# Gated cross-attention and mixture-of-experts block: three hand-written schedules re-ordered, and the running sum of softmax weights cut differently

## What is computed

```python
x = x + tanh(g_xattn) * cross_attention(layernorm(x), context)   # x: 4 x 512 x 512
x = x + tanh(g_ffn)   * moe_ffn(layernorm(x))
# cross_attention: q, k, v are linear maps, q and k RMS-normalised, 16 heads of 32;
#   two softmaxes, over 1344 text rows and over 257 image rows of the context,
#   their results summed, then a linear map
# moe_ffn: 8 experts (512 -> 2*256 -> 512), the two best of each token, weighted,
#   plus one shared expert (512 -> 2*1024 -> 512)
```

## Time and profile before

| | |
|---|---|
| median of 3 runs | 1726.33 us (1725.85 to 1728.0) |
| the profiled execution | 1728.0 us, its span from first to last instruction 1726.7 us |
| granted PE clock over the span | 0.997 |
| DVE busy | 1201.3 us (70%) |
| ACT busy | 822.3 us (48%) |
| POOL busy | 901.7 us (52%) |
| the DMA engines | 53% of the span, 158 GB/s |

### The profile page before, as it was taken

One profiled execution on the slowest core, in us unless ns is written; L12 is line 12 of the kernel. 1 busy time (PEld: TensorE's weight loads), 2 busy tenths in 40 slices (PEclk: granted clock), 3 DMA queues, 4 the chain that ended last, 5 costly groups with the idle time before them and its releaser, 6 DMA issues. The chain is left out here.

```text
span 1726.7 us, 24755 instructions
## 1 busy us (share of the span) xinstructions
PE 1689.0 (98%) x8694; PEld 1105.9 (64%) x8694; DVE 1201.3 (70%) x2250; ACT 822.3 (48%) x1520; POOL 901.7 (52%) x343
## 2 busy tenths in 40 slices
PE   6999999999999999999999999998999999999999
PEld 5888878885444445444544444445777778888777
DVE  6776677667888887888778888877555354443565
ACT  4433333236666664666556666662322355554221
POOL 3221312116777774787747777711515477675542
PEclk9999999999999999999999999999999999999999
DMA  9556858546555542554545445221313488876533
GB/s 330 165 165 196 229 182 211 180 164 192 138 151 146 145 134 57 147 151 132 148 122 127 111 131 142 84 93 42 134 37 134 159 266 271 261 264 211 166 109 98
DMA packets 198603, 273.04 MB, mean 158 GB/s; under 512 B 30968, under 2 KB 128008, under 8 KB 197964
## 3 DMA queue, kind: packets, MB, share of 16 engines
q1 hardware_dynamic: 192928, 254.61, 50.0%
q0 software_dynamic: 5120, 16.78, 2.9%
q10 hardware_dynamic: 432, 0.07, 0.0%
HBM read 198.15 MB, written 106.18 MB: 176 GB/s over the span
## 5 line engine op out<-in xcount | busy, mean ns | idle before, releaser
L1255 ACT ACTIVATE P<-ps 128x512 f32<-128x512 f32 (+1 forms) x832 | 444.4, 596 | 257.2 <-PE ps L1096 223.0
L640 DVE TENSOR_REDUCE mp<-ps 128x1 f32<-128x448 f32 x768 | 426.9, 613 | 83.9 <-PE ps L443 83.9
L1521 POOL TENSOR_TENSOR sacc<-sacc,P 128x2048 f32<-128x2048 f32 x90 | 396.3, 4403 | 17.5 <-ACT P L1255 6.9
L443 PE MATMUL ps<-Kst,Qst 96*128 96x448 f32 (+1 forms) x1024 | 382.6, 391 | 2.0 <-DVE mp L640 1.0
L443 PEld LDWEIGHTS ps<-Kst,Qst 96*128 96x128 f32 x1024 | 192.4, 188 | 210.8 <-DVE mp L640 150.5
L1096 PE MATMUL ps<-Qst,Kst 100*128 100x512 f32 (+1 forms) x832 | 321.2, 410 | 3.2 <-ACT P L1255 2.3
L1039 PE MATMUL ps<-P,Vg 128*32 128x512 f32 (+2 forms) x1664 | 216.2, 606 | 0.3 <-ACT P L1255 0.2
L822 POOL TENSOR_TENSOR cl<-craw,ch 128x1024 fp32r<-128x1024 f32 (+2 forms) x26 | 62.1, 2387 | 283.2 <-ACT ch L550 283.2
L1096 PEld LDWEIGHTS ps<-Qst,Kst 100*128 100x128 f32 (+1 forms) x832 | 151.8, 185 | 61.6 <-ACT P L1255 37.3
L49 PE MATMUL ps<-W,ch 128*128 128x512 f32 (+1 forms) x408 | 162.5, 398 | 0.0
L51 PE MATMUL ps<-W,cl 128*128 128x512 f32 (+1 forms) x408 | 159.7, 391 | 0.0
(11 more groups left out here) (245 smaller groups left out, 3072.0 us busy)
## 6 DMA issues: line engine op xcount, KB each, us to landing
gur<-in_w_gate_up SPq DMA_DIRECT2D x23, 1024.0 KB, 7.5
Kst<-KHd SPq DMA_DIRECT2D x56, 320.0 KB, 4.8
Vd<-vf SPq DMA_DIRECT2D x50, 256.0 KB, 2.1
craw<-in_ctxT SPq DMA_DIRECT2D x24, 512.0 KB, 4.5
KHd<-sth SPq DMA_DIRECT2D x24, 512.0 KB, 3.5
KLd<-stl SPq DMA_DIRECT2D x24, 512.0 KB, 4.8
dnr<-in_w_down SPq DMA_DIRECT2D x23, 512.0 KB, 3.9
xg<-Xg SPq DMA_DIRECT2D x23, 512.0 KB, 7.7
```

The lines of the kernel that those rows point to most:

```text
L443: pe.matmul(ps[:, bank, 0:c1 - c0], Qst[G % 3][0:96, j, 128 * qt:128 * qt + 128], Kst[G % 2][0:96, j, c0:c1], start=True, stop=True).then_ ...
L640: dve.reduce_max(out, ps[:, bank, 0:c1 - c0], AX.X).then_inc(d_ra, 1)
L1255: act.activation(P[slot(G, kt)][:m, j, :], ps[:m, 2 + (e - 1) % 3, :], ACT.Exp, scale=SCALE).then_inc(a_exp, 1)
L1521: pool.tensor_tensor(sacc[:, h], sacc[:, h], P[slot(G, kt)][:, h], ALU.add).then_inc(g_sum, 1)
```

## The change

- **Start of the projection.** On ACT, `weight_high` of the text keys' weights moves from `i = 1` to `i = 0`, ahead of `q_norm(0)`; that of the values' weights moves from ahead of `q_norm(2)` to behind `q_norm(1)`. On DVE, `ln_finish` and `centred` stand ahead of `q_add` in every iteration, and two `ln_stats` move behind `q_scale` and one iteration earlier.
- **Units.** One unit moves from step 7 to step 2 of each group.
- **Running sum.** POOL's first addition is one operation over four heads, not two over two heads each, and waits for the whole of tile 1; POOL adds two heads of tile 7 and DVE the other two (three and one before).
- **Feed-forward.** `gu_low` is four operations in place of one, `dn_low` two; the counts that others wait for follow. POOL no longer waits for `choose(3)` before `gu_low(3)` nor for the last `products` before `gu_low(4)`, and `dn_low(3)` stands behind `scatter(3)`.

```diff
@@ act_project, loop over i
             if i == 0:
                 chunk_high(0)
-            if i in (1, 2):
-                weight_high(i, s_wt[i - 1], W[:, 1, i - 1, 0], wraw[:, 1, i - 1, 1])
+                weight_high(1, s_wt[0], W[:, 1, 0, 0], wraw[:, 1, 0, 1])
             if i in (1, 3, 5, 9):
                 ln_root({1: 2, 3: 3, 5: 4, 9: 5}[i])
             if i < NT:
                 q_norm(i)
+            if i == 1:
+                weight_high(2, s_wt[1], W[:, 1, 1, 0], wraw[:, 1, 1, 1])
@@ dve_project, loop over i
             if i + 1 < NT:
                 x_low(i + 1)
-            if 1 <= i < NT:
-                q_add(i)
-            if 1 <= i < 7:
-                ln_stats(2 * i + 2)
-                ln_stats(2 * i + 3)
             if i + 3 < NT:
                 if i in (1, 3, 5, 9):
                     ln_finish({1: 2, 3: 3, 5: 4, 9: 5}[i])
                 centred(i + 3)
+            if 1 <= i < NT:
+                q_add(i)
             if i < NT:
                 q_variance(i)
             if 0 <= u < NU:
                 k_add(u)
             if i < NT:
                 q_scale(i)
+            if i < 6:
+                ln_stats(2 * i + 4)
+                ln_stats(2 * i + 5)
@@ attention
-    UNITS = (7, 6, 3, 6, 5, 6, 6, 6, 6, 5, 6, 2, 0)
+    UNITS = (7, 6, 4, 6, 5, 6, 6, 5, 6, 5, 6, 2, 0)
...
     def sum_no(G, kt):
-        return 8 * G + max(1, kt) + 1
+        return 7 * G + max(1, kt)
@@ dve_attend
-        def add_head_of_7(G):
+        def add_half_of_7(G):
             dve.wait_ge(a_exp, exp_no(G, 7, 3))
             dve.wait_ge(g_sum, sum_no(G, 6))
-            dve.tensor_tensor(sacc[:, 3:4], sacc[:, 3:4], P[slot(G, 7)][:, 3:4], ALU.add).then_inc(d_add, 1)
+            dve.tensor_tensor(sacc[:, 2:4], sacc[:, 2:4], P[slot(G, 7)][:, 2:4], ALU.add).then_inc(d_add, 1)
@@ pool_attend
-        def first_sum(G):
-
-            if G:
-                pool.wait_ge(p_tot, 5 * (G - 1) + TEXT_TOTAL)
-            for j in (0, 2):
-                pool.wait_ge(a_exp, exp_no(G, 1, j + 1))
-                h = slice(j, j + 2)
-                pool.tensor_tensor(sacc[:, h], P[slot(G, 0)][:, h], P[slot(G, 1)][:, h], ALU.add).then_inc(g_sum, 1)
-
         def add(G, kt):
             pool.wait_ge(a_exp, exp_no(G, kt, 3))
-            pool.wait_ge(g_sum, sum_no(G, kt) - 1)
-            h = slice(0, 3 if kt == 7 else 4)
-            pool.tensor_tensor(sacc[:, h], sacc[:, h], P[slot(G, kt)][:, h], ALU.add).then_inc(g_sum, 1)
+            if kt == 1:
+                if G:
+                    pool.wait_ge(p_tot, 5 * (G - 1) + TEXT_TOTAL)
+            else:
+                pool.wait_ge(g_sum, sum_no(G, kt) - 1)
+            h = slice(0, 2 if kt == 7 else 4)
+            pool.tensor_tensor(sacc[:, h], (P[slot(G, 0)] if kt == 1 else sacc)[:, h], P[slot(G, kt)][:, h], ALU.add).then_inc(g_sum, 1)
...
-            if G < NG - 1 and kt == 2:
-                first_sum(G)
-            if G < NG - 1 and 3 <= kt < 9:
+            if G < NG - 1 and 2 <= kt < 9:
                 add(G, kt - 1)
@@ pool_ffn
         def gu_low(q):
             pool.wait_ge(a_gu, q)
-            pool.tensor_tensor(gul[q % 2], gur[raw_slot(q)][:], guh[q % 2].bitcast(F32), ALU.subtract).then_inc(g_gu, 1)
+            for k in range(4):
+                pool.tensor_tensor(gul[q % 2][:, k], gur[raw_slot(q)][:, k], guh[q % 2][:, k].bitcast(F32), ALU.subtract).then_inc(g_gu, 1)
 
         def dn_low(q):
             pool.wait_ge(a_dn, q)
-            pool.tensor_tensor(dnl[q % 2], dnr[raw_slot(q)][:], dnh[q % 2].bitcast(F32), ALU.subtract).then_inc(g_dn, 1)
+            for k in range(2):
+                pool.tensor_tensor(dnl[q % 2][:, k], dnr[raw_slot(q)][:, k], dnh[q % 2][:, k].bitcast(F32), ALU.subtract).then_inc(g_dn, 1)
...
         scatter(2)
-        pool.wait_ge(d_run, 17)
         gu_low(3)
+        scatter(3)
         dn_low(3)
-        scatter(3)
-        pool.wait_ge(d_al, 16)
         gu_low(4)
```

More of the change, by code:

```diff
@@ L1428, in dve_attend @@
                 units(G + 1, at, sum(plan))
-                add_head_of_7(G)
+                add_half_of_7(G)
                 if more:
@@ L1636, in load_gu @@
                 sp.wait_ge(a_gu, raw_before(q))
-                sp.wait_ge(g_gu, raw_before(q))
+                sp.wait_ge(g_gu, 4 * raw_before(q))
             if 4 <= q < TAIL:
@@ L1649, in load_dn @@
                 sp.wait_ge(a_dn, raw_before(q))
-                sp.wait_ge(g_dn, raw_before(q))
+                sp.wait_ge(g_dn, 2 * raw_before(q))
             if 4 <= q < TAIL:
@@ L1709, in gate_or_up @@
                 pe.wait_ge(a_early, 3) if q == 0 else pe.wait_ge(a_gu, q)
-                pe.wait_ge(d_early, 3) if q == 0 else pe.wait_ge(g_gu, q)
+                pe.wait_ge(d_early, 3) if q == 0 else pe.wait_ge(g_gu, 4 * q)
             if z == 0 and i < 2:
@@ L1733, in down @@
                 pe.wait_ge(a_dn, q)
-                pe.wait_ge(g_dn, q)
+                pe.wait_ge(g_dn, 2 * q)
             pe.wait_ge(a_ah, 2 * z + 2)
@@ L1791, in rows_gate_up @@
                 pe.wait_ge(a_gu, q)
-                pe.wait_ge(g_gu, q)
+                pe.wait_ge(g_gu, 4 * q)
             if j < 2:
```

## The result

The changed kernel takes 1744.13 us in the median of four runs (1741.69 to 1747.21), the kernel before, on the same chip, 1727.16 us (1725.85 to 1728.19). The ratio is 1.0096 with a 95% interval of 1.0082 to 1.0109: the change costs 16.6 us. I had forecast 4.0 us and a range that ended at 1735.

What follows compares the result with a forecast made beforehand. PE, drawn busy for 98% of the span, was taken as the bound. From the profiled 1728.0, +3.0 - 0.4 + 1.7 - 0.3 gave 1732.0; that execution being 1.67 above the median, 1730.3 us, range 1722 to 1735.

Steps and rivals of the forecast that it cites:

- Part 1: Start of the projection: the new ACT and DVE order delays PE's fourth query projection from 29.43 to 32.4, +3.0 us.
- the uncertain term: Start of the projection: PE keeping full clock through the new stops gives +1.8, a second half-clock stretch +4.0.
- Part 2: Attention: moving one unit from step 7 to step 2 gains 0.43 us a group by itself.
- Part 3: Attention's running sum: the late sum on POOL covers the unit's gain in plain groups; together with the unit -0.4 us.
- 0.06 is left: End of each attention group: DVE's extra 0.53 on tile 7 is hidden by 0.47 idle time, leaving +0.06.
- Rival (c): Attention: DVE's additions set each group's end because ACT's copy moves too; 14 x 0.5 = +7, 1737.5 us; chance 0.11.
- the lateness of the whole first addition: Attention: POOL's sixth whole addition ends at 571.79, so tile 10's first exponential starts at 571.85, not 570.5.
- Part 4: Feed-forward: prefix sums stop PE about 3.0 us, the stop at 1317.62 goes: +1.7, with -0.3 for the other pieces.
- let one operation of `choose(3)` through each time: Feed-forward: each of four POOL pieces' ends admits one DVE operation, so the six-operation chain ends near 1315.9, not 1311.7.
- meet no matmul that waits for them: Feed-forward: `dn_low(3)` behind the scatter and the earlier `gu_low(4)` delay no waiting matmul; priced at nothing.
- the -0.3 for shorter holds by pieces: Feed-forward: the other pieces hold DVE more briefly, gaining 0.3 us for `al` in the last steps.

Runs made afterwards that it cites:

- e1: Kernel before with only the new order at the start of the projection, on ACT and DVE: ratio 1.0018, +3.1 us.
- e4: Kernel before with only one unit moved from step 7 to step 2: ratio 0.9958, -7.3 us.
- e9: Kernel before with the moved unit and half of tile 7 added on DVE, first sum still two half additions: ratio 0.9997, -0.5 us.
- e2: Kernel before with the moved unit and the whole running-sum change: ratio 1.0025, +4.3 us.
- e10: Kernel before with the running-sum change alone (whole first addition, half of tile 7 on DVE), units unmoved: ratio 1.0034, +5.9 us.
- e3: Kernel before with the feed-forward change alone (pieces, two waits gone, other order): ratio 1.0065, +11.2 us.
- e14: Kernel before with only POOL's wait for the 17th run, ahead of `gu_low(3)`, removed: ratio 1.0034, +5.9 us.
- e7: Changed kernel with POOL's wait for the 16th `al` put back ahead of `gu_low(4)`: ratio 1.0093 to the kernel before, +16.1 us.
- e15: Kernel before with the feed-forward change alone, but the wait for the 17th run back ahead of `gu_low(3)`: ratio 1.0035, +6.0 us.
- e5: Kernel before with POOL's low parts in pieces only, both waits and old order kept: ratio 1.0007, +1.2 us.
- e8: Changed kernel with each POOL piece waiting for the piece before it, opening gaps: ratio 1.0075 to the kernel before, +13.0 us.

## Why the prediction was wrong

**Part 1, right.** Forecast +3.0 us, fourth query projection at 32.4; it measured +3.1 us (e1) and stands at 32.64. That the idle time is moved and not removed holds too. The clock was the uncertain term and stays one: it falls in some of these executions and not in others. The close number is partly luck: e1's trace kept its full clock, for which the forecast had +1.8, and from the second query projection to the transposes behind the first keys it takes 22.62 us where before takes 20.90, 1.7 more; in the changed kernel's trace, where the clock fell, it is 24.20, 3.3 more.

**Part 2, right.** -0.43 us a group was the unit's worth; e4 gives 7.3 us over 14 groups, 0.52 each, and 0.5 in the group shown.

**Part 3, wrong in one term.** Forecast -0.4 us with part 2, measured +4.3. The step that failed is "0.06 is left" of the half addition's 0.53 on DVE. It measured 6.8 us over 14 groups (e9 less e4), 0.49 each by time and 0.4 by the traces' groups, nearly all of it. Rival (c) had named it: ACT's `mrh`, the copy that DVE waits for, moves as well. I let the 0.47 us of DVE's idle time stand against it although that idle time is itself a wait for something DVE had delayed. The row that says so, [0.23 <-DVE sacc L1383] at 577.83, was in the trace of before. The other term, the lateness of the whole first addition, was right. Tile 10's first exponential was to stand at 571.85, 39.73 us behind `mrh` (532.12 in before); it stands 39.72 us behind it (577.00 and 537.28). In the forecast's sum this lateness eats the gain of the plain groups, some 4.8 us (-0.4 less -6.0 for the unit and less 0.8 for the ends of the groups); e2 less e9 is 4.8. So the miss of part 3 is the half addition, 6.0 us above the forecast, less the 1.3 us by which the unit was worth more than I had it. The path was longer than I had it, through PE's score matmuls and DVE's maxima, and what comes next I hadn't looked at: tile 11's first exponential overwrites tile 7, and by my own numbers POOL's half of tile 7 would end at 571.79 + 0.14 + 2.39 = 574.32, where that exponential stands at 572.82 + 0.98 = 573.80. The wait is there (0.46 us at 579.52); it doesn't set the group's length, since in e10, with the same wait, DVE's addition is as late as in before.

**Part 4, wrong, and the largest miss.** Forecast +1.4 us, measured +11.2 (e3). The mechanism that failed is that four pieces "let one operation of `choose(3)` through each time". The row of 1405.22 showed one such boundary, and I made it a rule. In the changed kernel no boundary let the cast go, and it was held for the whole row of four; the cast, with its one input, isn't even among the six operations that I counted. For the stop itself that made little difference: 3.69 us in place of 3.0. The Trainium skill ("SBUF — State Buffer", Who interferes with whom) says that a DVE instruction with two SBUF inputs, or a cast in a mode that uses both port pairs, contends with a GpSimd instruction that reads SBUF, and that the one that issues second is blocked for the whole of the first; the hold of 4.79 us by one operation (e14) agrees in its length, and a hold through four operations in a row is more than it says. The microseconds were lost in two terms that I put at nothing. One is the clock behind the stop, 1.6 to 2.9 us in the two traces, though I had priced the same thing in part 1; with both, one removed wait costs 5.9 us (e14) where +1.7 stood. The other is "meet no matmul that waits for them": `dn_low(3)` behind the scatter meets `al`, for which a down product's third tile waits, 2.3 us in e7 and e15, with 1.5 us of half clock behind it in e15; with the smaller steps that follow, and with the pieces (+1.2 alone), that is 6.0 us (e15) where 0 stood. Last, the -0.3 for shorter holds by pieces has nothing to show for it (e5).

Two slips in the sums changed nothing: part 3 counts 15 groups (12 and 3) where 14 are taken elsewhere, and (c) has 1737.5 where 1730.3 + 7 is 1737.3.

The direction "slower" had the larger chance, 0.47, but for a size of 4 us. The range ended at 1735 because (c) was cut off and part 4 was bounded at +2.5; the bound came from counting one DVE operation a boundary, not from asking what PE's clock and the operations moved to the scatter's far side cost.

## What to carry to other kernels

An idle time can only hide a delay if what ends it isn't moved by the same delay: follow the wait back one more step before you count it as cover. A wait that seems to cost an engine's time may be what keeps its long operation away from another engine's chain of small ones; before it is removed, or an operation is moved past a queue of others, list what the other engine does there and who waits for that. A stop of PE is priced with the slow matmuls that come behind it. And pieces only let others in where there is a gap between them.

## What the runs showed of the hardware that was not expected

- **Who gets in between two POOL operations.** I went through the traces of before, of the changed kernel and of all fifteen experiments behind attention, and took each DVE operation that was over 0.2 us longer than the shortest of its kind and under way when one POOL subtraction ended and the next followed. Where the next was drawn from 0.03 to 0.07 us before the end of the last, DVE was let through at 25 boundaries and not at 22. Where there was a gap of 0.02 to 0.08 us between them, it was let through at all 6. At the two places that mattered (the cast; `al` behind `dn_low(3)`) it was 0 of 17 without a gap. The same `al` two steps earlier got through between two pieces (e5: `al` of 1.62 us at 1315.90, while POOL's row of three pieces from 1314.43 took 4.24 us in place of 3.8). What decides without a gap stays open.
- **The order of the starts does not tell who is held.** The cast begins 0.17 us before POOL's operation in the changed kernel and in e14 and is the one that is held. The same page of the Trainium skill has it that who issues first gets the ports; by the recorded starts it is here the other way round, so a small DVE operation that starts just ahead of a POOL operation isn't safe.
- **A stop of 3.06 us (e8) left PE at full clock, one of 3.29 us (e14) and one of 3.69 us (the changed kernel) did not**; in e14 the granted clock was 0.50 from 1317.00 to 1321.90. A shorter one, 2.26 us, did not either (e15, 0.50 from 1336.20). At the start a stop of 2.21 us was followed by half clock in before, and one of 2.20 us at the same place was not in e4 (granted clock 1.00 from 28.97 to 43.00 of its trace). So the length of the stop alone doesn't tell, and what a stop costs differs from one execution of the same code to the next.
- **A releaser can be misnamed.** At 577.00 of the changed kernel the row names PE for a wait that ends with POOL's addition at 576.91. In e2 the same wait is put down to POOL (1.30 us, at 572.52).
